# First attention of a two-layer network: gate folded into the value weights, values copied by ScalarE, second layer's modulation placed after the slot table

## What is computed

```python
ca, sa, ga, cb, sb, gb = modulation(silu(c) @ wmod)      # six vectors of 128
h = layernorm(x) * (1 + ca) + sa
q, k, v = h @ WQ, h @ WK, h @ WV
score = (q @ k.T) / sqrt(128) * band                     # band of 64; zero outside, not minus infinity
x = x + ga * (softmax(score) @ v)
h = layernorm(x) * (1 + cb) + sb
x = x + gb * experts(h)                                  # 2 of 16 experts per token, 128 -> 512 -> 128
```

## Time and profile before

| What | Value |
|---|---|
| Median of 3 runs | 506.08 us (505.69 to 508.32) |
| Profiled execution, its own time | 501.9 us |
| Span of the profiled execution | 500.2 us |
| PE busy | 421.4 us (84%) |
| DVE busy | 362.5 us (72%) |
| ACT busy | 280.8 us (56%) |
| POOL busy | 253.4 us (51%) |

### The profile page before, as it was taken

One profiled execution on the slowest core, in us unless ns is written; L12 is line 12 of the kernel. 1 busy time (PEld: TensorE's weight loads), 2 busy tenths in 40 slices (PEclk: granted clock), 3 DMA queues, 4 the chain that ended last, 5 costly groups with the idle time before them and its releaser, 6 DMA issues.

```text
span 500.2 us, 11175 instructions
## 1 busy us (share of the span) xinstructions
PE 421.4 (84%) x2573; PEld 316.4 (63%) x2573; DVE 362.5 (72%) x1185; ACT 280.8 (56%) x753; POOL 253.4 (51%) x340
## 2 busy tenths in 40 slices
PE   3979762396999999569999999999897969999994
PEld 3567651296999998236556556656554556777774
DVE  5859884052665666489999999999966536777774
ACT  2447540142555554277888888888655245665551
POOL 4014767031545445425545686785666027666562
PEclk9999955597999999799999999999999999999998
DMA  8912425666677686662142161000001321222217
GB/s 230 283 14 56 72 65 116 134 155 166 169 191 209 182 260 203 157 177 72 33 106 68 48 166 55 11 23 11 13 23 43 98 64 46 76 78 80 62 50 227
DMA packets 62321, 53.67 MB, mean 107 GB/s; under 512 B 9677, under 2 KB 51710, under 8 KB 62131
## 3 DMA queue, kind: packets, MB, share of 16 engines
q1 hardware_dynamic: 55330, 42.97, 33.4%
q0 software_dynamic: 5056, 8.48, 5.1%
q10 hardware_dynamic: 1872, 1.52, 1.3%
HBM read 41.15 MB, written 13.73 MB: 110 GB/s over the span
## 4 chain that ended last, share of the span: by engine, by line
PE 28%; DVE 25%; issue 16%; POOL 9%; SPq 9%; DMA 8%; ACT 4%; DVEq 0%; POOLq 0%; ACTq 0%
POOL results L854 6%; PE bank L1847 4%; PE bank L1800 3%; DVE qk_sums L1422 3%; PE bank L1906 3%; PE bank L1815 3%; DVE sums L1445 3%; POOL sorted_tokens L839 3%; PE bank L1946 2%; DVE big L1415 2%; DVE work L1459 2%; SPq L592 2%; SPq L678 2%; DMA results<-work 2%; DMA big<-in_W 2%
## 5 line engine op out<-in xcount | busy, mean ns | idle before, releaser
L854 POOL DMA_INDIRECT results<-work x94 | 92.3, 982 | 96.1 <-DVE work L1379 67.7
L1847 PE MATMUL bank<-late,work 128*128 128x512 f32 x192 | 92.6, 612 | 2.6 <-ACT work L1014 2.4
L990 ACT ACTIVATE work<-bank,mcol 128x128 f32<-128x128 f32 x94 | 43.0, 457 | 72.7 <-PE bank L1792 72.7
L1359 DVE TENSOR_SCALAR work<-bank,b_columns 128x128 f32<-128x128 f32 x94 | 28.7, 347 | 35.9 <-PE bank L1800 35.8
L1847 PEld LDWEIGHTS bank<-late,work 128*128 128x128 f32 x192 | 33.7, 195 | 32.5 <-issue 29.1
L1800 PE MATMUL bank<-work,big 128*128 128x128 f32 x376 | 53.3, 288 | 0.0
L1815 PE MATMUL bank<-big,work 128*128 x376 | 51.0, 280 | 0.1
L1800 PEld LDWEIGHTS bank<-work,big 128*128 128x128 f32 x376 | 49.1, 204 | 0.1
L1815 PEld LDWEIGHTS bank<-big,work 128*128 128x128 f32 x376 | 47.1, 197 | 0.3 <-issue 0.3
L999 ACT ACTIVATE work<-bank,b_columns 128x128 f32<-128x128 f32 x94 | 29.4, 363 | 29.1 <-PE bank L1800 29.1
L1792 PE MATMUL bank<-ident,work 128*128 128x128 f32 x94 | 27.0, 287 | 18.5 <-DMA work<-sorted_tokens 10.2
(11 more groups left out here) (254 smaller groups left out, 1003.5 us busy)
## 6 DMA issues: line engine op xcount, KB each, us to landing
big<-in_W SPq DMA_DIRECT2D x47, 256.0 KB, 2.7
work<-sorted_tokens SPq DMA_DIRECT2D x94, 65.0 KB, 1.9
big<-in_w SPq DMA_DIRECT2D x48, 88.0 KB
big<-results SPq DMA_DIRECT2D x14, 256.0 KB, 3.7
sorted_tokens<-zeros SPq DMA_DIRECT2D x26, 65.0 KB, 2.6
late<-in_WqkvbT SPq DMA_DIRECT2D x1, 1544.0 KB
results<-work POOLq DMA_INDIRECT x94, 2.9
bias_big<-in_b1e SPq DMA_DIRECT2D x16, 88.0 KB
```

Of the source, the lines that this page charges most:

```text
L854: pool.indirect_dma_start(ys[l], bass.IndirectOffsetOnAxis(xg[b][:, D:D + 1].bitcast(I32), 0), yo[b], None, bounds_check=TOPK * T - 1, oob ...
L990: act.activation(xgT[b % 2], bank[:, ends[b % 2], 0:P], ACT.Identity, bias=scale_shift[0], scale=scale_shift[1]).then_inc(e_xTc, 1)
L1847: last = pe.matmul(bank[:, 2 * k + i, :], h3T[b], Wqkvb[:, k * HD + i * 512:k * HD + (i + 1) * 512], start=True, stop=True)
```

## The change

1. DVE multiplies the value weights `Wa[:, 2]` by the first gate once. Values and outside products come out of PE gated. PE's first value group waits for this and stands one step later, as the second does.
2. `values(g)` becomes a copy and goes to ACT, at steps 1, 2, 5 and 7 (DVE had them at 0, 1, 5 and 6).
3. Two of the four outside rows (g = 0, 1) go to ACT, steps 3 and 4; DVE keeps the others (steps 8 and 14). The memsets of the counts go to POOL.
4. The second layer's modulation leaves step 16. PE makes it after the slot table's last product, DVE after the slot table.

Core of the diff (`last_values` and some semaphore counts left out):

```diff
             def ends_ready(half):
+                pool.memset(ends_of[half][0:2 * BAND + 1, :, D:D + 1], float(T - WIN)).then_inc(a_tail, 1)
+                pool.wait_ge(a_tail, (3, 8)[half])
                 pool.memset(ends_of[half][0:2 * BAND, :, D:D + 1], 1.0).then_inc(a_tail, 1)
...
+            def values(g):
+                act.wait_ge(a_vp, g + 1)
+                act.copy(V[:, 4 * g:4 * (g + 1), 0:D],
+                         bank[:, (4, 5, 7, 7)[g], :].rearrange("p (i n) -> p i n", i=4)).then_inc(a_v, 1)
+
+            def outside_rows(g):
+                act.wait_ge(a_w, g + 1)
+                act.activation(ends_of[0][2 * BAND:2 * BAND + 1, 4 * g:4 * g + 4, 0:D],
+                               bank[2 * BAND:2 * BAND + 1, 6 + g, :].rearrange("p (i n) -> p i n", i=4),
+                               ACT.Copy, scale=-1.0).then_inc(a_wr, 1)
+
             def beside(s):
+                if s in (3, 4):
+                    outside_rows(s - 3)
                 if s in (4, 5, 10):
                     keys({4: 1, 5: 2, 10: 3}[s])
+                if s in (1, 2, 5, 7):
+                    values({1: 0, 2: 1, 5: 2, 7: 3}[s])
...
-            def values(g):
-                dve.wait_ge(a_vp, g + 1)
-                dve.tensor_tensor(V[:, 4 * g:4 * (g + 1), 0:D],
-                                  bank[:, (4, 5, 7, 7)[g], :].rearrange("p (i n) -> p i n", i=4),
-                                  gB[:, 0, 0, :].unsqueeze(1).to_broadcast([P, 4, D]), ALU.mult).then_inc(a_v, 1)
...
             gate_vectors(6, 0, 1)
+            dve.wait_ge(ld_attn, 48)
+            dve.tensor_tensor(Wa[:, 2, :], Wa[:, 2, :], gB[:, 0, 0, :], ALU.mult).then_inc(s_mod_ready, 1)
...
-                elif s == 16:
-                    dve.wait_ge(s_mod, 3)
-                    columns(1)
-                    gate_vectors(2, 1, 4)
...
             count_real_slots(0)
+            dve.wait_ge(s_mod, 3)
+            columns(1)
+            gate_vectors(2, 1, 4)
...
-                if s == 0:
+                if s == 1:
+                    pe.wait_ge(s_mod_ready, 3)
                     value_group(0)
-                elif s == 1:
+                elif s == 2:
                     value_group(1)
-                elif s == 2:
                     pe.wait_ge(a_hs, NT // 4 + 3)
                     outside_products(0)
...
-                elif s == 16:
-                    pe.wait_ge(a_wr, 6)
-                    pe.wait_ge(ld_c1, 16)
-                    mod_row(2, 0, 1)
-                    mod_row(2, 1, 0)
-                    mod_row(2, 1, 1)
-                    mod_columns(1).then_inc(s_mod, 1)
...
             turn_slots(0)
+            pe.wait_ge(a_wr, 4)
+            pe.wait_ge(ld_c1, 16)
+            mod_row(2, 0, 1)
+            mod_row(2, 1, 0)
+            mod_row(2, 1, 1)
+            mod_columns(1).then_inc(s_mod, 1)
             pe.wait_ge(t_ready, 1)
```

More of the change, by code:

```diff
@@ L568, in build @@
         d_xT, d_h, d_q, d_k, d_v, d_b = sem("d_xT"), sem("d_h"), sem("d_q"), sem("d_k"), sem("d_v"), sem("d_beta")
-        DS, TAILS = 9, 4 + NT // 4
+        DS, TAILS = 9, 6 + NT // 4
         d_eb = sem("d_exp_beta")
@@ L1181, in gate_vectors @@
                                               -1.0, gtmp[:, 0, c, :], ALU.add, ALU.mult))
-            def values(g):
-                dve.wait_ge(a_vp, g + 1)
-                dve.tensor_tensor(V[:, 4 * g:4 * (g + 1), 0:D],
-                                  bank[:, (4, 5, 7, 7)[g], :].rearrange("p (i n) -> p i n", i=4),
-                                  gB[:, 0, 0, :].unsqueeze(1).to_broadcast([P, 4, D]), ALU.mult).then_inc(a_v, 1)
             def last_values():
                 dve.wait_ge(a_vp, NT // 4 + 1)
-                dve.tensor_tensor(V[0:2 * BAND, NT, 0:D], bank[0:2 * BAND, 2, 0:D],
-                                  gB[0:2 * BAND, 0, 0, :], ALU.mult).then_inc(a_v, 1)
+                dve.wait_ge(a_v, NT // 4)
+                dve.tensor_copy(V[0:2 * BAND, NT, 0:D], bank[0:2 * BAND, 2, 0:D]).then_inc(a_v, 1)
             def scaled(g):
@@ L1243, in outside_rows @@
             def outside_rows(g):
-                half = g // 2
                 dve.wait_ge(a_w, g + 1)
[L1247 to L1253, removed]
+                dve.tensor_scalar(ends_of[1][2 * BAND:2 * BAND + 1, 4 * (g % 2):4 * (g % 2) + 4, 0:D],
+                                  bank[2 * BAND:2 * BAND + 1, 2, :].rearrange("p (i n) -> p i n", i=4),
+                                  -1.0, None, ALU.mult).then_inc(a_wr, 1)
             def beside(s):
@@ L1384, in _ @@
             dve.wait_ge(ld_w0, 32 + 16 * E)
-            dve.wait_ge(s_mod_ready, 5)
+            dve.wait_ge(s_mod_ready, 6)
             experts = table(mybir.EngineType.DVE, tbl, P, E - 1)
@@ L1678, in beside @@
                     key_group(1)
-                    pe.wait_ge(a_wr, 3)
+                    pe.wait_ge(a_wr, 2)
                     value_group(2)
@@ L1690, in beside @@
                 elif s == 10:
-                    pe.wait_ge(a_wr, 5)
+                    pe.wait_ge(a_wr, 3)
                     key_group(3)
@@ L1736, in attend @@
                     pe.wait_ge(a_v, g + 2)
-                    pe.wait_ge(a_wr, g + 2 + g // 2)
-                    pe.wait_ge(a_tail, (4, 5, 7, TAILS)[g])
+                    pe.wait_ge(a_wr, g + 1)
+                    pe.wait_ge(a_tail, (5, 6, 9, TAILS)[g])
                 after(pe, b_x, t)
```

13 lines of the change are left out of this document (4 added, 9 removed).

## The result

| | Kernel before | Changed kernel |
|---|---|---|
| Median | 506.27 us (505.69 to 508.32, 4 runs) | 500.43 us (498.18 to 501.72, 4 runs) |
| Profiled execution, its own time | 501.9 us | 498.18 us |
| Span | 500.2 us | 496.4 us |
| Ratio | | 0.9899, 95% interval 0.9851 to 0.9946 |

The medians differ by 5.8 us, the profiled executions by 3.7. Forecast were 7.6 and a time of 498.5. Executions of one kernel scatter by up to 13 us (before: 499.2 to 512.1 in that comparison). The ratios leave out each kernel's runs over 1.5% above its fastest, so for kernels that scatter this much a ratio and the medians can disagree by a per cent.

What follows compares the result with a forecast made beforehand. POOL's queue of sends was taken to bound the start of the first slot, with all later work shifting whole. Savings of 1.9 + 3.1 + 2.6 = 7.6 us off the 506.08 median gave 498.5 us, range 495.2 to 503.0.

Steps and rivals of the forecast that it cites:

- POOL as a queue that pays each wait in full: Attention loop to first slot: POOL's sends start 1.27 us apart, and every wait of POOL before 67.05 delays the end.
- Front: Start of the attention stage: ACT's copies and fewer DVE operations bring sends 1.9 us earlier, bounds -0.6 and 2.5.
- Modulation out of the loop: From the third pair on POOL never waits; its 24 sends need 29.2 us instead of 32.3, saving 3.1 us.
- Landing: Last send lands in 4.0 us instead of 6.6, most of the DMA pile being gone; saving 2.6, bounds 0 and 4.3.
- Modulation behind the table: Moved modulation behind the slot table is hidden by 4 us and costs nothing; bias columns near 83.6, first turn 87.6.
- The clock at 1.00 up to the loop's end: Expected sign: PE keeps full clock until the attention loop's end near 71, counted as 1.0 us of that end's shift.
- A block that shifts whole: Everything after 95 us follows from the first slot's start and moves earlier by the same amount.
- Landing long: Rival: sends keep 6.6 us landing because zero rows and first weights still pile up; saving 5.0, 501.1 us; chance 0.13.
- ACT takes the saving back: Rival: in the front, waits on DVE become waits on ACT; saving 5.7, 500.4 us; chance 0.09.
- POOL held: Rival: two operations of DVE's chain each block a send of POOL; saving 6.5, 499.6 us; chance 0.05.
- Given back later: Rival: slots wait for SP's weight transfers; half the saving lost gives 502.3, all 506; chance 0.08.
- Clock falling in the front: Rival: ACT's queue idles PE, the dense stretch from 38 to 60 runs at half clock, +10 us, 508.5; chance 0.04.

Runs made afterwards that it cites:

- e1: Kernel before with only the second layer's modulation moved from step 16 to behind the slot table; 503.66 us against 506.29, ratio 0.9943.
- e2: Changed kernel with the second layer's modulation put back at step 16 on DVE and PE; 506.05 us against 506.29, ratio 1.0035.
- e3: Changed kernel with value copies and all four outside rows back on DVE, gate still folded into the value weights; 503.32 us, ratio 0.9939.
- e8: Changed kernel with SP's two first weight transfers behind its wait for all sends and zero rows; 501.81 us against 506.89, ratio 0.9996.
- e7: Changed kernel with the second layer's gate chain computed twice behind the slot table; 499.41 us in one run.
- e6: Kernel before run once more, unaltered; 508.62 us, span 506.9.
- e12: Kernel before with two one-column memsets added on DVE ahead of its first group of scaled tiles; 505.84 us against 507.64, ratio 1.0076.
- e5: Changed kernel with seven one-column memsets added on DVE behind the second layer's gate vectors; 497.82 us against 506.89, ratio 0.9904.
- e10: Changed kernel with three added memsets on DVE where e5 has seven; the second layer's tiles 0 to 15 took 143.26 us.
- e9: e5 with the weights of slot 8 and on issued behind the same slot's tokens, eight transfers earlier; 493.80 us against 503.66, ratio 0.9833.
- e4: Changed kernel run once more, unaltered; 502.48 us against 506.29, ratio 0.9925.

## Why the prediction was right, and where it was not

**What bounds the kernel.** POOL as a queue that pays each wait in full: right up to the first slot, shown by e1 and e2. Each removes its wait, and the effects add up there.

**Front, 1.9 us.** Measured 2.55 at the third pair (53.81 to 51.26). The term was too small: the fourth value group came at 28.45, not 29.3, since the groups ahead of it had moved up as well, and ACT's copy ended at 28.39. e3 shows that ACT's copying, not the folded gate, makes it. The wait on the multiply and the bound of -0.6 didn't come up.

**Modulation out of the loop, 3.1 us.** Measured 2.73 (32.30 to 29.57); left were waits put down to issue, such as 0.52 at 56.57. The last send at 80.83, forecast 81.1: the front's 0.65 too little and these 0.37 too much nearly cancel.

**Landing, 4.0 us.** Measured 5.21, so 1.4 us saved instead of 2.6. This is the mis-sized term of the start. I counted the pile of zero rows as the only company and had the rest through by 83.6; the first weights also move earlier with the table (78.32), and e8 puts 1.6 us on them. With them away it is 3.57. The pile itself began at 73.47 and not at 72.8.

**Modulation behind the table, nothing.** Right: bias columns at 82.77, forecast 83.6, and e7 hides twice the chain. The first turn at 88.43, forecast 87.6. By row, 0.2 us were priced for a send beside DVE's chain, and none showed: the sends at 80.83 here and at 82.12 in e7 took 0.97 us. But that was no test of the row. In the loop the longer send ran beside the chain's last operation, L1180, the only one of 384 columns that reads two SBUF tensors; it came again in each trace that has the chain there (1.14 or 1.15 us in before, e2, e6 and e12), while the sends beside the other operations took 0.97. In the new place that operation begins at 82.17, after the last send's 81.80 (83.49 after 83.09 in e7), so no send met it. By the rule of the Trainium skill (page "SBUF — State Buffer", section "SBUF: two separate sides") the chain would lock GpSimd out if its operations ran in a two-port mode. Whether they did no row tells; the four sends of the loop were longer by some 0.17 us, of the 0.3 us that they shared with the operation, and in the new place nothing bears on the rule either way. (A send of 1.05 us at 62.92 in the changed kernel has no such chain beside it.)

**The clock at 1.00 up to the loop's end.** Wrong. It fell between 63 and 64 in the changed kernel too. I had tied that fall to the 3.64 us of PE idling alone; the longest wait in the 4 us ahead of it was now 0.88 us. It did not hold up the sends, which POOL sets and not PE; the loop's end came 7.25 us earlier (first zero rows 80.72 to 73.47) instead of the 7.9 that counted 1.0 for a full clock.

**"A block that shifts whole" behind 95.** This is the step that failed. By it 6.75 us at the first turn should have been 6.75 in the span; they became 3.8. Shown: 1.2 us go to the gaps on DVE, which show because the change takes instructions out of DVE's stream (e5, e10). Another 0.5 us stand at the first tile, which varies by more than that between executions. The other 2.9 us go, in the profiled execution, to two falls of the clock; they were there in most traces with gaps and rare at the first place without them, but e9 has them too, so their cause is not settled. 1.7 us came in on the way, in the slots, where the ninth slot waits for weights in every kernel of the study but e9 (2.24 to 5.26 us by trace); in e4 the same stretch lost 1.4 us instead, so this part is scatter.

**The rivals.** Landing long: half of it came true. ACT takes the saving back: no. POOL held: no. Given back later: this happened, and not by the transfers that I named. Clock falling in the front: not with the change, but in e1 and e3, where PE's wait remains: 3.0 us at the first send, not the +10 that I had put on it. The condition that I gave for a fall, only beyond 2 us of idling, was wrong: 2.0 us were enough in three executions and not in three others. The range held the result because it was built on the start's bounds alone and the losses behind it happened to be of the same size as its upper part. That is luck.

## What to carry to other kernels

Price a change at the place where it acts, but then check the block behind it tile by tile against the old trace before calling it shifted: here 1.2 us in three steps of 0.24 to 0.47 stood in code nobody had touched. Where an engine shows a small gap "issue" at one instruction after instructions were removed far ahead of it, pad with a few cheap ones in a place with slack and look whether the gap moves. The version with seven memsets was 4.0 us under e8, the nearest to the bare change in the same comparison, and with the weights' order of e9 the ratio to the kernel before was the best measured, 0.9833.

## What the runs showed that I had not expected

A gap of 0.20 to 0.26 us on DVE that belongs to a position in its instruction stream, one place in 128: with seven memsets gone from this loop, with three moved to the instruction ahead. The granted clock falls behind waits of PE of 1.4 to 2.0 us in some executions and kernels and not in others with the same wait; behind the one in the front it cost 3.0 us. A faster start can bring such a fall: in e4 and e5 the slots ran at full clock from 93 to 95 us on, where the changed kernel's first trace had half up to 97, met the late weights after 5.2 us of waiting instead of 2.9, and fell to half clock behind it.
